# Experts' token slots in blocks of 384 and of 256 instead of blocks of 384 alone

## The reference, cut to what matters

```python
x = hidden_states.reshape(-1, D)                 # T = 8192, D = 256
logits = x @ wr.T                                # E = 8
vals, idx = jax.lax.top_k(logits, TOP_K)         # TOP_K = 2
...
gating = jax.nn.softmax(sparse, axis=-1)
cap = max(8, int(max(1, T * TOP_K // E) * CAP_FACTOR))   # 2560
...
xg = x_pad[dispatch]
h = _gelu(jnp.einsum('ecd,edf->ecf', xg, w1) + b1[:, None, :])
y = jnp.einsum('ecf,efd->ecd', h, w2) + b2[:, None, :]
wy = y * g[..., None]
out = jax.ops.segment_sum(wy.reshape(-1, D), dispatch.reshape(-1), num_segments=T + 1)[:T]
```

## Time and profile before

| | |
|---|---|
| median of three runs | 952.57 us (951.37 to 953.0) |
| profiled execution | 954.04 us, span 952.0 us |
| instructions | 19269 |
| TensorE matmul busy | 932.3 us, 98% of the span |
| ScalarE busy | 537.6 us, 56% |
| VectorE busy | 470.6 us, 49% |
| GpSimd busy | 409.4 us, 43% |
| DMA | 82.18 MB, mean 86 GB/s |

### The profile page before, as it was taken

How to read it: one execution, slowest core, us unless ns; L and a number is a source line. 1 busy time by engine, 2 the same in 40 slices (tenths; PEclk the granted TensorE clock), 3 DMA queues, 4 the chain that set the end, 5 groups by cost and what they waited for, 6 DMA issues and landing times.

```text
span 952.0 us, 19269 instructions
## 1 busy us (share of the span) xinstructions
PE 932.3 (98%) x6447; PEld 892.4 (94%) x6448; DVE 470.6 (49%) x1084; ACT 537.6 (56%) x1223; POOL 409.4 (43%) x419
## 2 busy tenths in 40 slices
PE   8999999999999999999999999999999999999994
PEld 5666799999999999999999999999999999999994
DVE  4488867546444454346444454455444543443441
ACT  5888554656555565456555655556555555555551
POOL 0000214636545445445445455355355355455443
PEclk9999999999999999999999999999999999999998
DMA  9566293352622342323522353225223223223223
GB/s 332 182 223 224 74 343 66 53 129 52 138 34 52 51 125 50 48 40 51 133 43 47 45 133 48 41 50 134 39 51 45 39 51 47 37 52 50 34 34 33
DMA packets 53559, 82.18 MB, mean 86 GB/s; under 512 B 6736, under 2 KB 42576, under 8 KB 53136
## 3 DMA queue, kind: packets, MB, share of 16 engines
q0 software_dynamic: 26496, 36.76, 24.3%
q1 hardware_dynamic: 25472, 44.44, 13.9%
q10 hardware_dynamic: 1552, 0.53, 0.2%
HBM read 54.17 MB, written 35.93 MB: 95 GB/s over the span
## 4 chain that ended last, share of the span: by engine, by line
PE 96%; DVE 1%; ACT 1%; DMA 1%; issue 0%; POOL 0%; SPq 0%; DVEq 0%; POOLq 0%
PE bank L565 14%; PE bank L566 14%; PE bank L567 14%; PE bank L552 14%; PE bank L553 14%; PE bank L554 13%; PE bank L461 5%; PE bank L542 3%; PE bank L509 2%; PE bank L474 2%; PE bank L476 2%; DMA sb_w<-in_w 1%; ACT sb_hid_t L702 0%; POOL out_rows L386 0%; ACT sb_x L667 0%
## 5 line engine op out<-in xcount | busy, mean ns | idle before, releaser
L734 ACT ACTIVATE sb_h_raw<-bank,sb_b_now 128x384 f32<-128x384 f32 x368 | 215.0, 584 | 282.8 <-PE bank L554 266.3
L1083 DVE TENSOR_TENSOR sb_h_lo<-sb_h_raw,sb_h_hi 128x384 fp32r<-128x384 f32 x368 | 204.9, 557 | 296.4 <-ACT sb_h_hi L734 287.0
L565 PE MATMUL bank<-sb_w_hi,sb_h_hi 128*128 128x256 f32 x1104 | 315.1, 285 | 0.0
L566 PE MATMUL bank<-sb_w_lo,sb_h_hi 128*128 128x256 f32 x1104 | 310.8, 282 | 0.0
L567 PE MATMUL bank<-sb_w_hi,sb_h_lo 128*128 128x256 f32 x1104 | 310.1, 281 | 0.0
L386 POOL DMA_INDIRECT out_rows<-sb_y,sb_add_ids x138 | 233.5, 1692 | 89.9 <-DVE sb_y L1106 54.8
L552 PE MATMUL bank<-sb_xt_hi,sb_w_hi 128*128 128x384 f32 x736 | 249.6, 339 | 0.5 <-ACT sb_h_hi L734 0.5
L554 PE MATMUL bank<-sb_xt_hi,sb_w_lo 128*128 128x384 f32 x736 | 248.8, 338 | 0.0
L553 PE MATMUL bank<-sb_xt_lo,sb_w_hi 128*128 128x384 f32 x736 | 248.8, 338 | 0.0
L734 ACT ACTIVATE sb_h_hi<-bank,sb_b_now 128x384 fp32r<-128x384 f32 x368 | 212.8, 578 | 0.0
L566 PEld LDWEIGHTS bank<-sb_w_lo,sb_h_hi 128*128 128x128 f32 x1104 | 208.2, 189 | 0.0
(11 more groups left out here) (136 smaller groups left out, 597.0 us busy)
## 6 DMA issues: line engine op xcount, KB each, us to landing
sb_w_raw<-in_w SPq DMA_DIRECT2D x16, 1024.0 KB
hidden<-sb_rows SPq DMA_DIRECT2D x4, 2112.0 KB, 9.6
sb_x<-in_x_t SPq DMA_DIRECT2D x16, 512.0 KB, 4.7
out_rows<-in_x SPq DMA_DIRECT2D x16, 512.0 KB, 6.4
sb_xg<-hidden,sb_gather_ids POOLq DMA_INDIRECT x138
out_rows<-sb_y,sb_add_ids POOLq DMA_INDIRECT x138
sb_b<-in_b SPq DMA_DIRECT2D x1, 1024.0 KB, 8.9
hidden<-sb_empty SPq DMA_DIRECT2D x3, 132.0 KB, 8.4
```

Source lines behind the costliest of these rows:

```text
L565: pe.matmul(y, hi, w_hi[u][:, cols], start=(f == 0 and s != 1), stop=False, skip_group_check=True)
L566: pe.matmul(y, hi, w_lo[u][:, cols], start=False, stop=False, skip_group_check=True)
L734: ins = act.activation(h, h_bank[f % H_BANKS][:, 0:SLOTS], ACT.Gelu_apprx_tanh, bias=b1_now[u][:, f:f + 1])
L1083: dve.tensor_tensor(h_lo[f % RING][:, :], h_raw[f % RING], h_hi[f % RING][:, :].bitcast(F32), ALU.subtract).then_inc(h_ready, 1)
```

## The change

Expert 0 keeps its blocks of 384 slots. Each of the others gets first long blocks of 3 tiles and then short blocks of 2 tiles (`SHORT` = 2), in numbers that `BLOCKS_FOR` gives for its count of tiles, at least 3 long and 2 short. With the token counts above these are 3+4, 3+4, 4+3, 3+3, 3+4, 4+3 and 4+2 for experts 1 to 7: with expert 0's 5 there are 29 long and 23 short blocks, 52 in all, 133 tiles.

- TensorE, the gelus, `split_chunk`, `add_bias` and `weigh` do two tiles in a short block. `split_rows` (L709, L1069) is not touched: it still copies 384 columns a half.
- GpSimd still issues three gathers and three adds for each block. The third gather of a short block has 16 rows (`FEW_ROWS`), all of them spare rows, and its list takes four copies instead of two. `adds(b)` inside both loops is called without `subs`, so it still has three DMAs of 128 rows; only the last two blocks' third add has 16 rows.
- Each expert of 1 to 7 has two inner loops on each engine instead of one, and `plan_of` gives three numbers.
- `plan_blocks` works on tables of 20 steps for each expert instead of 7; one more pad tile is cleared in `hidden` and in `out_rows`.

```diff
+SHORT = 2
+FEW_ROWS = 16
+LEAST = 5
+LONG_LEAST = 3
+BLOCKS_FOR = {13: (3, 2), 14: (3, 3), 15: (3, 3), 16: (4, 2), 17: (3, 4), 18: (4, 3), 19: (5, 2), 20: (4, 4)}
...
-PAD = SUBS * P
+PAD = (SUBS + 1) * P
...
+            all_three = eng.value_load(plan[0:1, bass.ds(e, 1)], min_val=0)
+            before = all_three // 256
+            return before, before + all_three % 16 + LONG_LEAST, before + all_three // 16 % 16 + LEAST
...
-            def list_block(k, tile):
-
-                block_ids = ids[:, bass.ds(tile, SUBS)]
-                pool.tensor_copy(gather_ids[:, :], block_ids)
-                pool.tensor_copy(ids_ring[:, bass.ds((k % 4) * SUBS, SUBS)], block_ids).then_inc(gather_listed, 1)
-
-            def gather(sets=SETS):
+            def list_block(k, tile, subs=SUBS):
+
+                block_ids = ids[:, bass.ds(tile, subs)]
+                pool.tensor_copy(gather_ids[:, 0:subs], block_ids)
+                if subs < SUBS:
+                    pool.tensor_copy(gather_ids[:, subs:], spare_row[:, :])
+                    pool.tensor_copy(ids_ring[:, bass.ds((k % 4) * SUBS + subs, 1)], spare_row[:, :])
+                pool.tensor_copy(ids_ring[:, bass.ds((k % 4) * SUBS, subs)], block_ids).then_inc(gather_listed, 1)
+
+
+            def gather(sets=SETS, subs=SUBS):
                 for s in range(SUBS):
+                    n = P if s < subs else FEW_ROWS
                     pool.indirect_dma_start(
-                        xg[:, s, :], None, hidden[0:PAD + sets * TS * P, :],
-                        bass.IndirectOffsetOnAxis(gather_ids[:, s:s + 1], axis=0),
+                        xg[0:n, s, :], None, hidden[0:PAD + sets * TS * P, :],
+                        bass.IndirectOffsetOnAxis(gather_ids[0:n, s:s + 1], axis=0),
                     ).then_inc(gathered, 16)
 
-            def adds(b):
+            def adds(b, subs=SUBS):
...
+                    n = P if s < subs else FEW_ROWS
...
-                with pool.Fori(start, start + both % 16 + LEAST) as b:
-                    next_block(b + LAG, e * TILES_E + (b - start) * SUBS + EARLY_TILES)
+                start, short_at, end = plan_of(pool, e + (E + 1))
+                tile = e * TILES_E + EARLY_TILES
+                with pool.Fori(start, short_at) as b:
+                    next_block(b + LAG, tile + (b - start) * SUBS)
+                    adds(b)
+                tile = tile + (short_at - start) * SUBS
+                with pool.Fori(short_at, end) as b:
+                    next_block(b + LAG, tile + (b - short_at) * SHORT, subs=SHORT)
                     adds(b)
             rest = all_blocks(pool, less=1)
             for i in range(LAG):
-                adds(rest + i)
+                adds(rest + i, SHORT)
...
-            def first_product(u, f):
-
-                h = h_bank[f % H_BANKS][:, 0:SLOTS]
+            def first_product(u, f, subs=SUBS):
+
+                h = h_bank[f % H_BANKS][:, 0:subs * P]
...
-            def second_product(u, f):
+            def second_product(u, f, subs=SUBS):
...
-                for s in range(SUBS):
+                for s in range(subs):
...
+                    if f == FC - 1 and s > 0:
+                        mm.then_inc(y_done, SUBS - subs + 1)
...
-            def expert(u, e, start, end):
-                with pe.Fori(start, end - 1) as b:
+            def expert(u, e, start, short_at, end):
+                with pe.Fori(start, short_at - 1) as b:
                     one_block(u, u, b)
+                one_block(u, u, short_at - 1, subs_next=SHORT)
+                with pe.Fori(short_at, end - 1) as b:
+                    one_block(u, u, b, subs=SHORT, subs_next=SHORT)
...
-            def gelu(u, b, f):
+            def gelu(u, b, f, subs=SUBS):
...
+                    ins = act.activation(h[:, 0:subs * P], h_bank[f % H_BANKS][:, 0:subs * P], ACT.Gelu_apprx_tanh,
...
-            def split_chunk(b, f):
-
+            def split_chunk(b, f, subs=SUBS):
+
+                cols = slice(0, subs * P)
...
+            def signals(s, subs):
+                return SUBS - s if s == subs - 1 else 1
+
+            def add_bias(e, b, s, subs):
...
-                for s in range(SUBS):
-                    add_bias(e, b, s)
+                for s in range(subs):
+                    add_bias(e, b, s, subs)
```

More of the change, by code:

```diff
@@ L64 @@
 OPEN = 2
[L65 removed]
+assert ROWS == 512 and T % (4 * ROWS) == 0 and CAP % P == 0 and max(BLOCKS_FOR) == FULL and 3 * COLS <= 512
 WCOLS = KC * F
@@ L324, in _ @@
             sp.wait_ge(set_dve, 1)
-            for s in range(SUBS):
+            for s in range(PAD // P):
                 sp.dma_start(hidden[s * P:(s + 1) * P, :], empty_sb[:, :]).then_inc(pad_zero, 16)
@@ L637, in _ @@
             pe.wait_ge(plan_ready, 1)
-            _, end = plan_of(pe, 0)
-            expert(0, 0, EARLY, end)
+            _, _, end = plan_of(pe, 0)
+            with pe.Fori(EARLY, end - 1) as b:
+                one_block(0, 0, b)
+            one_block(0, 1, end - 1, PIECES * 2)
             with pe.Fori(0, E // 2 - 1) as pair:
@@ L749, in bias, with expert @@
                 act.wait_ge(bias_now, e + 1)
-            def expert(u, e, start, end):
+            def expert(u, e, start, short_at, end):
                 for j in range(2):
                     one_block(u, e, start + j, j * len(SPLIT_AT))
-                with act.Fori(start + 2, end) as b:
+                with act.Fori(start + 2, short_at) as b:
                     one_block(u, e, b, None)
+                if short_at is not end:
+                    with act.Fori(short_at, end) as b:
+                        one_block(u, e, b, None, subs=SHORT)
             bias(0, 0)
@@ L766, in _ @@
                     bias(u, e)
-                    start, end = plan_of(act, e)
-                    expert(u, e, start, end)
+                    start, short_at, end = plan_of(act, e)
+                    expert(u, e, start, short_at, end)
             bias(1, E - 1)
-            start, end = plan_of(act, E - 1)
-            with act.Fori(start, end - 1) as b:
+            start, short_at, end = plan_of(act, E - 1)
+            with act.Fori(start, short_at) as b:
                 one_block(1, E - 1, b, None)
-            one_block(1, E - 1, end - 1, None, last=True)
+            with act.Fori(short_at, end - 1) as b:
+                one_block(1, E - 1, b, None, subs=SHORT)
+            one_block(1, E - 1, end - 1, None, last=True, subs=SHORT)
         @block.vector
@@ L1150, in _ @@
                     e = pair * 2 + (2 - u)
-                    start, end = plan_of(dve, e)
-                    expert(u, e, start, end)
-            start, end = plan_of(dve, E - 1)
-            with dve.Fori(start, end - 1) as b:
+                    start, short_at, end = plan_of(dve, e)
+                    expert(u, e, start, short_at, end)
+            start, short_at, end = plan_of(dve, E - 1)
+            with dve.Fori(start, short_at) as b:
                 one_block(1, E - 1, b, None)
-            one_block(1, E - 1, end - 1, None, last=True)
+            with dve.Fori(short_at, end - 1) as b:
+                one_block(1, E - 1, b, None, subs=SHORT)
+            one_block(1, E - 1, end - 1, None, last=True, subs=SHORT)
 def constants():
@@ L1162, in constants @@
     tile = np.arange(TILES_E)
-    more_than = np.arange(BLOCKS) * SLOTS
+    more_than = np.arange(FULL) * P
     earlier = np.arange(E)[None, :] < np.arange(E + 1)[:, None]
-    least = np.where(np.arange(E) == 0, FIRST_LEAST, LEAST)
+    least = min(BLOCKS_FOR)
+    blocks = np.array([(a + b - LEAST, a - LONG_LEAST) for a, b in (BLOCKS_FOR[max(n, least)] for n in range(FULL + 1))])
+    adding = np.tile(np.diff(blocks, axis=0).T[:, None, :], (1, E, 1))
+    adding[:, 0, :] = np.arange(FULL) % SUBS == 0
     slot_pos = p[:, None] + P * tile[None, :]
```

174 lines of the change are left out of this document (91 added, 83 removed).

## The result

The changed kernel takes 994.08 us (median of four runs, 992.43 to 995.41) against 952.18 us (four runs, 951.37 to 953.0) on the same chip: ratio 1.0442, 95% interval 1.0427 to 1.0457. It is 41.9 us slower. The forecast was 969.5 us in a range of 956 to 988: the direction is right, the size is not.

What follows compares the result with a forecast made beforehand. TensorE bound the kernel before; in short blocks GpSimd's lap (15.25 us against 12.5) would. Terms -27.0 + 13.2 + 27.8 + 3 - 0.5 + 0.5 = +17.0 on the 952.57 us median gave 969.6, stated as 969.5, range 956 to 988.

Steps and rivals of the forecast that it cites:

- TensorE's work, -27.0: TensorE's blocks: 23 short ones of 11.9 us replace 17 long ones of 17.69 us, -27.0 us.
- The copies, +13.2: Short blocks: TensorE waits 0.6 us for the rows' 384-column copies, in 22 blocks, +13.2 us.
- The lap of 15.25: GpSimd's lap beside a short block: 15.25 us, 2.75 more than TensorE's 12.5, third gather taken at 0.5.
- rival 3: GpSimd's gathers: 16 rows cost as much as 128, lap 15.7, +23 us in all, 976 us; chance 0.2.
- The waits, +27.8: TensorE's waits for gathers in short runs: six second blocks at 0.5 us, nine later ones at 2.75, +27.8 us.
- +3 for loops: GpSimd's loop switches: at 0.25 to 0.5 us each, six runs start about 0.5 us later, +3 us (0 to 15).
- Rival 4: GpSimd's loop switches at the bound, 13 of 2.2 us each, +15 us more, 985 us; chance 0.1.
- rival 5: TensorE's clock: some waits grow, one chunk at half speed after each of nine waits, +13 us, 983 us; chance 0.08.
- Front and end: Two more small clears in the front, +0.5 us; at the end smaller last adds and uncovered first bias, -0.5 in all.

Runs made afterwards that it cites:

- two_both: Changed kernel with two gathers and two adds in short blocks, and (3,4) instead of (4,2) for the last expert: 957.39 us.
- defer: Changed kernel with GpSimd's wait for its adds to land moved behind the next lap's gathers; all gathers and adds stay: 952.30 us.
- xt256: Changed kernel with `split_rows` copying 256 columns instead of 384 where block and next block are short (16 blocks): 995.98 us.
- few128: Changed kernel with 128 rows instead of 16 in the third gather of a short block: 995.21 us.
- fill: Changed kernel with 32 unread matmuls before TensorE's wait for gathers in the last short block of experts 1 to 6: 992.41 us.
- unroll: Changed kernel with TensorE's loop over pairs of experts written out: 992.19 us.
- last_four: two_both with 256-column copies where block and next block are short, and (4,2) again with three adds for the last expert: 946.07 us.
- two_gathers: Changed kernel with two gathers instead of three in short blocks and one list copy less; the adds stay: 973.05 us.
- defer_all: defer with 256-column copies where both blocks are short (16 blocks) and TensorE's loop over pairs written out: 940.89 us.
- last_unroll: last_four with TensorE's loop over pairs of experts written out: 939.31 us.
- xt_two: two_gathers with copies of 256 columns instead of 384 in 16 short blocks: 976.36 us.

## Why the prediction was right and wrong

**TensorE's work, -27.0: right.** 14.12 us into a run and 12.47 per short block with its copies' wait (two_both, defer) are the forecast of 14.1 and 12.5.

**The copies, +13.2: right in kind, 11.0 in size.** 0.50 us each where 0.6 was taken, 21 of them between the first and the last transposes and one behind. xt256 shows that it was worth nothing to remove while the lap was the bound.

**The lap of 15.25: right by luck in its parts.** Measured 15.16 and 15.32. The third gather was put at 0.5 and took 0.85. This was rival 3. The Trainium skill, "DMA: Bandwidth & Descriptors", "Anatomy of one DMA — SWDGE (gpsimd) path", says that descriptor generation adds little until there are many: few128 agrees (0.95 us for 128 rows, 0.85 for 16). The page's fixed 2 us include the completion; what GpSimd itself is busy with for 16 rows is 0.85 us for a gather and 1.3 for an add. The four copies of lists and the time around them came out shorter than the prediction's 0.4 us more (1.49 us from the first copy to the first gather instead of 1.28), and made up for most of it.

**The waits, +27.8 and +3 for loops, 30.8 together: 37.9.** For experts like the first the count was near (0.72 + 2.90 + 1.89 = 5.5 where 6.0 were forecast). At expert 2 GpSimd was late by 5 us once more: 8.46 us of idle time before the first copy of its short run, where other laps have 3.5.

```profile
360.89 0.44 POOL L381 COPY sb_gather_ids<-sb_ids 128x2 int32 x1 [8.46 <-issue]
```

Its four waits are 2.17, 2.20, 2.77 and 3.27 us, 10.4 together. Rival 4 had such lateness at 13 switches of 2.2 each; it came once, with 5. In fill and unroll it comes at expert 4 as well (6.84 and 8.17 us before the first copy).

**The step that failed: the clock.** The prediction left it out of the sum ("My waits of 2.75 us are shorter than that idle time") and kept it as rival 5 with 0.08 and +13 for nine falls of one chunk each. Measured: eight stretches, 34.2 us at half clock, about 15.6 us of TensorE's time. It is the largest term that the sum lacked. The span grew by 24.2 us more than forecast: 15.6 for the clock, 7.1 for the waits, 4.6 for code, -2.2 for the copies, -3.3 for the front and +2.6 for the end give 24.4. The 15.6 are what passed at the low clock, not what the kernel would gain without it: in fill 10.3 us of speed gave 1.7. The mechanism stood there, but the trace of before had only one idle time of TensorE to judge it by, at the end, and from one long wait nothing follows for shorter ones: a bound with it inside should have been part of the range. The falls came behind waits of 2.65 to 3.9 us here and of 1.84 in last_four, but not behind 2.17 and 2.20 at 384.95 and 399.80, nor behind 3.05 at 313.72 in two_gathers: the length of the wait alone doesn't tell. The Trainium skill, "TensorE: Matmul & The Clock Gate", Part 1, says that activity lifts the clock; the trace agrees, since in fill matmuls whose result nobody reads kept it up (13.6 us at half clock instead of 34.2). What fill adds is that the clock was not the root: keeping it up gave 1.7 us at most, taking away the waits (defer) 41.8.

**A term that was not thought of: code, +4.6.** Two waits of 2.1 us where TensorE's loop over pairs jumps back. The kernel before has the same loop and no such wait, with less code in it; its q8 queue moved 16 packets of 0.26 MB, the changed one's 41 and 0.67 MB. In time they fit: in the blocks of unroll its packets lie 12 us or more apart everywhere, in the changed kernel everywhere but around the two waits (four packets from 432 to 452 us, four from 648 to 664). That this queue's packets are what TensorE waits for, and that the loop's length decides, is argued from this and from unroll (36 packets, no wait), not shown.

**Front and end.** Up to the first transposes the kernel is 2.8 us faster, not 0.5 slower; the same part took 129.5 us in defer and 131.8 in defer_all, so it moves with the code in a way that I can't explain. The last two 16-row adds saved 0.2 us each, not half of 0.9:

```profile
972.06 1.55 POOL L404 DMA_INDIRECT out_rows<-sb_y,sb_add_ids  x1 [0.31 <-issue]
973.91 1.34 POOL L404 DMA_INDIRECT out_rows<-sb_y,sb_add_ids  x1 [0.30 <-issue]
```

**Shown and open.** Shown: the lap of GpSimd is the cause of the slowdown (defer takes back 41.8 us by changing its last wait alone, two_gathers 21 by one small gather a lap), and it pulls the clock down with it (34.2 us at half clock become 3.4 in defer). Open: what the low clock costs by itself while the lap is the bound, why the two waits of "issue" come, why GpSimd is late at expert 2, 2 us of fill, the front, and the longer end.

## What to carry to other kernels

Before shrinking a block, sum the lap of each engine that serves it, with the landing that it waits for, and compare that with the new block: 43% busy was a lap of 15.3 us beside a block of 12.5. A wait at the end of a lap for a DMA's landing is the first thing to move; here that one step was worth as much as all the savings in issues (defer_all 940.89, last_unroll 939.31). And once TensorE must wait again and again, count its clock too: 35 us of waits brought 34 us at half speed, and shorter work on TensorE (xt_two) made both longer.

## What the runs showed of the hardware that was not expected

- A gather of 16 rows issued from GpSimd takes 0.85 us, one of 128 rows 0.95 to 0.98; an add of 16 rows 1.34 against 1.55 to 1.63.
- A clock that falls behind a wait makes the wait dearer where nothing else is the bound: two waits of 1.84 and 1.89 us in last_four, about 4 us with what is hidden, each with 3.4 us at half clock behind it, were worth 6.8 us in the median. While GpSimd's lap was the bound, keeping the clock up was worth 1.7 us at most (fill, where the intervals overlap).
- In these kernels a jump back over two experts' code on TensorE goes with a wait of 1.8 to 2.6 us that no releaser explains; written out straight, the same code runs without it. The kernel before has the jump with less code and no such wait.
